# GpSimd's gathers of five passes wait for the sum three turns back in place of four

## The reference

```
agg = segment_sum(edge_attr, dst);  x = LN(x + x + W2 softplus'(W1 agg))          # layer 0
neigh = segment_sum(x[src]*ew, dst) / max(ws, 1)
x = LN(x + (x Wself + neigh Wneigh + b)/2)                                       # layer 1
x = LN(x + relu(x w_s + segment_sum((x w_n)[src], dst)))                         # layer 2
h = relu(cheb(x; T0, T1 = lap(x), T2 = 2 lap(lap(x)) - x))                       # layer 3
x = LN(x + cheb(h))
lap(h) = segment_sum(w * h[src], dst)
```

## Time and profile before

| what | us |
|---|---|
| median of 3 runs (4736.85 to 4740.95) | 4739.85 |
| the profiled execution, its own time | 4710.22 |
| its span, first to last instruction | 4708.4 |
| L1, from its first gather to that of L2 | 327.0 |
| L2 | 313.5 |
| T1 | 315.6 |
| T2 | 319.8 |
| LH | 325.4 |
| LU, to the end | 567.2 |

### The profile page before, as it was taken

One profiled execution on the slowest core, in us unless ns is written; L12 is line 12 of the kernel. 1 busy time (PEld: TensorE's weight loads), 2 busy tenths in 40 slices (PEclk: granted clock), 3 DMA queues, 4 the chain that ended last, 5 costly groups with the idle time before them and its releaser, 6 DMA issues. The chain is left out here.

```text
span 4708.4 us, 74947 instructions
## 1 busy us (share of the span) xinstructions
PE 3333.1 (71%) x20670; PEld 2616.6 (56%) x20670; DVE 3087.9 (66%) x12832; ACT 2498.5 (53%) x7359; POOL 3171.7 (67%) x3630
## 2 busy tenths in 40 slices
PE   2266986777999999999995664666868878831111
PEld 0023655665888888888884564653436667721111
DVE  2277996997888888888885775771213434545544
ACT  0002776997888888888884552114545643311111
POOL 6402767885888888888885664656656646566776
PEclk6598998998999999999997777888999988955555
DMA  0003663664222222222222443435657766632332
GB/s 21 4 1 92 185 178 123 214 215 149 78 76 75 77 78 78 76 75 78 78 78 67 127 134 100 134 123 176 227 176 255 268 205 209 215 111 91 90 88 70
DMA packets 311878, 575.84 MB, mean 122 GB/s; under 512 B 69502, under 2 KB 97975, under 8 KB 311466
## 3 DMA queue, kind: packets, MB, share of 16 engines
q1 hardware_dynamic: 235178, 443.56, 28.0%
q0 software_dynamic: 76288, 127.51, 10.1%
HBM read 301.23 MB, written 271.14 MB: 122 GB/s over the span
## 5 line engine op out<-in xcount | busy, mean ns | idle before, releaser
L561 POOL DMA_INDIRECT rows<-state,rows_of_src x588 | 555.8, 945 | 390.5 <-issue 155.0
L844 DVE TENSOR_TENSOR_SCAN x<-same,x,ps 128x512 f32<-128x512 uint8 x336 | 429.0, 1277 | 319.2 <-PE ps L1360 205.2
L1360 PE MATMUL ps<-ident,rows 128*128 128x128 f32 x1372 | 287.2, 316 | 460.9 <-ACT rows L1130 250.0
L1113 ACT ACTIVATE yTa<-ps 128x512 f32<-128x512 f32 x392 | 232.8, 594 | 602.8 <-PE ps L1342 338.7
L561 POOL DMA_INDIRECT rows<-lap,rows_of_lap x392 | 383.4, 978 | 218.2 <-issue 109.9
L1360 PEld LDWEIGHTS ps<-ident,rows 128*128 128x128 f32 x1372 | 202.2, 165 | 510.7 <-issue 304.6
L645 POOL DMA_INDIRECT lk<-node_table,look_idx x392 | 388.9, 992 | 92.2 <-issue 84.1
L1130 ACT ACTIVATE rows<-rows,lap_w 128x128 f32<-128x128 f32 (+1 forms) x784 | 269.6, 418 | 278.0 <-DMA rows<-lap,rows_of_lap 211.1
L1118 ACT ACTIVATE sd<-mv,consts 128x4 f32<-128x4 f32 x588 | 174.6, 297 | 438.0 <-DVE mv L856 172.9
L1498 PE MATMUL ps<-V,hT 128*128 128x128 f32 x3136 | 403.2, 282 | 5.0 <-ACT hT L1249 5.0
L960 DVE BATCH_NORM_STATS2 bn<-y 128x6 f32<-128x128 f32 x1764 | 379.6, 278 | 23.3 <-POOL y L597 23.2
(11 more groups left out here) (259 smaller groups left out, 9473.4 us busy)
## 6 DMA issues: line engine op xcount, KB each, us to landing
state_h<-hb SPq DMA_DIRECT2D x98, 512.0 KB
xin<-in_x_dram SPq DMA_DIRECT2D x196, 256.0 KB
out_dram<-outb SPq DMA_DIRECT2D x196, 256.0 KB
xe<-state SPq DMA_DIRECT2D x147, 256.0 KB
state<-outb SPq DMA_DIRECT2D x98, 256.0 KB
state<-oe SPq DMA_DIRECT2D x98, 256.0 KB
h_pre<-hb SPq DMA_DIRECT2D x49, 512.0 KB
rows<-in_edge_attr_10x_dram SPq DMA_DIRECT2D x48, 320.0 KB
```

What stands on the lines that cost most here:

```text
L561: gp.indirect_dma_start(out=dest[:, at, k, 0:width], out_offset=None, in_=table_, in_offset=bass.IndirectOffsetOnAxis(ap=index[:, c:c + 1] ...
L844: v.tensor_tensor_scan(t[0:np_, g.b].rearrange("p k d -> p (k d)"), same[0:np_, 512 * g.c:512 * g.c + 512], ps[0:np_, bk + g.b, :], t[0:np ...
L1360: i = t.transpose(bank(g.b)[:, k, :], rows[:, g.r, k, 0:P], ident[:, :])
```

## The change

One number: in the passes L1, L2, T1, T2 and LH turn g's gathers wait for `summed` of turn g - 3, not g - 4. The four buffers stay. Turn g writes buffer g modulo 4 as before, so the new wait is stricter than what the buffer needs. LU, tgt0 and src0 are as they were.

```diff
             def edge_pass(p, table_, index, width=P):
                 enter(pool, p)
-                run_turns(QUADS, 0, lambda g: gather(p, g, table_, index, rows, g.r, width, rows_in, [(summed, RING)]))
+                run_turns(QUADS, 0, lambda g: gather(p, g, table_, index, rows, g.r, width, rows_in, [(summed, 3)]))
                 leave(pool)
```

## The result

| | us |
|---|---|
| before, median of 7 runs | 4738.60 |
| after, median of 7 runs (4706.15 to 4724.60) | 4720.86 |
| after / before | 0.9960, 95% interval 0.9944 to 0.9975 |
| predicted | 4718.5 |

What follows compares the result with a forecast made beforehand. POOL's gathers, with stops for PE's late-seen sums, were taken as the bound. Start -27.0, middle +29.9, end -24.3 sum to -21.4 us, taking 4739.85 to 4718.5; by itself 4708 to 4730, overall range 4708 to 4747.

Steps and rivals of the forecast that it cites:

- The cause of the stall: At pass starts, POOL's unbroken gathers hold PE's signals; four passes stop after 24 gathers and restart at about 34 us.
- the first rival: At pass starts, the stall has a cause other than POOL's gathers, so the restart stays put: 4740 us, chance 0.19.
- the backlog: In POOL's unbroken gathers, a queue said to hold PE's signals until drained; each further gather costs 1.35 us.
- The start: First stall of each pass: POOL stops four gathers earlier, release comes 5.4 us sooner; five passes save 27.0 us.
- the middle: From restart to last turn: one more turn of each pass runs at the coupled pace, +29.9 us in all.
- the end: After each pass's last gather: one turn fewer remains at PE's own pace, -24.3 us in all.
- POOL and PE keep their rhythm: In the middle of each pass: same rhythm, only with gathers one turn less ahead; the added coupled turns cost +29.9 us.
- the second rival: In L2, T1 and T2, two turns and a stop become one turn and a stop: 12 us cost, 4730.5, chance 0.07.
- Rows in time: At LH's weighing, rows need 7.55 us and have 8.5 us of cover; that leaves 1 us, cost taken 0.
- The third rival: At ACT's weighing in LH and L1, rows come late: 4750 to 4790 us, chance 0.11.

Runs made afterwards that it cites:

- e1: The change as it is (three turns back in the five passes) against the kernel before, on another chip: 1.0006 (0.9997 to 1.0016).
- e7: Kernel before (four turns back), with PE's four products of each sum in the five passes done three times over: 1.0189 of the kernel before.
- e8: Three turns back, with PE's four products of each sum in the five passes done three times over: 1.0185 of the kernel before.
- e10: Only the sixth turn of each pass waits three back, all others four, against the kernel before (4699.0 us): 0.9991 (0.9981 to 1.0001).
- e12: First twelve turns of each pass wait four back, from the thirteenth three back, against the kernel before (4746.2 us): 0.9983 (0.9971 to 0.9995).
- e9: Kernel before (four turns back) plus two small POOL settings behind each gather of the five passes, against the kernel before (4699.0 us): 1.0039.
- e11: Kernel before (four turns back) plus four small POOL settings behind each gather of the five passes, against the kernel before (4746.2 us): 1.0057.
- e6: All five passes wait two turns back, against the kernel before, on a prompt chip: 1.0312 (1.0294 to 1.0331).

## Why the prediction came out, point by point

**The cause of the stall** held on the chip where it was made. Signals of PE are late because POOL issues DMAs without a break: this was argued from four times of 34 us. The change itself bears it out, since the restart moved with the count in all five passes, 27.1 us in sum for 27.0 (in T2 to 33.6 us, after 24 gathers), and with that the first rival fell there. The loop beside the puts shows the lateness where nothing joins the two engines. That the signals come through once POOL is silent and the backlog drained is one step too much: beside the puts they come through every 28 us or oftener with POOL going on, and what holds them stays open. And the rival holds on the other chips (e1, e7, e8), and that a chip might be of another kind was in none of my cases.

**The start, the middle and the end belong together**: e10 has the early restart without the rest, and gives at most 9 us; the whole change gives 0.4%. But e12, which should have cost 0 to 12 us, gained 2 to 14. On its chip about 8 us are there without the start, where the whole change gave 18 on the first, by a gain in LH that my sum doesn't have.

**"POOL and PE keep their rhythm"** is the step that was off, in both directions, and hence the middle's +29.9 us, which measured +42.5. A turn more is 5.0 us of gathers and whatever the stops change. POOL's waits from the restart to the last turn, before and then after, in L1:

```profile
POOL rows L561 <- PE ps L1360: 43.4, 17, 4.4
POOL rows L561 <- remote: 13.0, 6, 4.3
```

```profile
POOL rows L561 <- PE ps L1360: 52.0, 17, 4.0
...
POOL rows L561 <- remote: 15.4, 9, 3.8
```

and in LH:

```profile
POOL rows L561 <- remote: 41.1, 28, 4.4
...
POOL rows L561 <- PE ps L1364: 25.9, 12, 3.5
```

```profile
POOL rows L561 <- remote: 51.1, 38, 2.1
...
POOL rows L561 <- PE ps L1364: 11.8, 5, 4.1
```

L1 has 56.4 us of stops before and 67.4 after: 11.0 + 5.0 = 16.0 us, where I had 6.1. LH has 67.0 and 62.9: -4.1 + 5.0 = 0.9, where I had 6.2. In LH before, each of the five stretches of two turns ends in a stop of 1.7 to 1.9 us and the turn behind it in one of 2.2 to 3.2, among single turns with 1.0; after, 42 of 44 stretches of gathers are single turns. That is the second rival's mechanism, and I had priced it as a loss, from the earlier trace rows and for other passes (12 us; with the 4.69 + 1.28 = 5.97 us that stand there it would be 14 to 15). In LH, where most turns were single already, it was a gain of 5.3 us. e12 shows it again, and e9 with four turns back, so that it goes with the rhythm rather than with the distance. What makes a pass settle in single turns is not shown. L1's loss of 9.9 us is not settled: its turn took 6.10 and 6.03 us with four back (before, e10) and 6.33 and 6.60 with three (after, e12). But these are single executions of several chips, and with four back and the settings it took 6.31 in e11 and 6.5 in e9. So L1 differs by as much from trace to trace without the change, and its +9.9 can't be put down to it.

**The end** was sized within a tenth in sum, -26.7 for -24.3, by errors that cancel: L1 had 0.9 us less than its term, T1 and T2 1.3 and 2.0 more.

**Rows in time**: nearly right for three back. The 1 us of slack in LH was read well, and it was used up: from the restart on ACT has 12 waits ahead of its weighing in after, 10.5 us in sum and none above 1.3, where before it had none. The pass became shorter all the same. The third rival's place was thus right. With two turns back (e6, on a prompt chip) late rows cost 138 us in the passes; that L1 would fall deepest was not seen.

The errors of the middle (+12.6) and the end (-2.4) leave the trace at -11.3 us for -21.4. The medians say -17.7, with an interval of -12 to -27; -21.4 lies in it, and the sum of this one pair of traces, which may be of two chips, just outside. The profiled execution did not go from 4710.2 to 4688.8 us but to 4724.6, with 24.3 us of the difference ahead of L1. And no pass did what was forecast for it: each should have been 4 to 5 us shorter. LH gained 9.0 by something that the sum has not, L1 lost 6.8, the other three gained about 3 each. That 4720.9 stands so close to 4718.5 is luck; the mechanism of the start and of the end is not.

## What to carry to other kernels

When a consumer resumes long after its producer's record has ended, and a third engine that issues indirect DMAs falls silent just before, look for a loop elsewhere in the trace that shares no data with that engine: if it slows as well, the signal is held and the work is not late. A shorter wait at one place alone gains nothing, since it is eaten at the next turn. Look at the rhythm too: what a pass gains can come from pairs of turns that break up into single ones, and a sum of mean turns doesn't see that. Don't read a pass's gain of some us off one pair of traces: L1, four turns back (with POOL's settings and without), took from 325 to 348 us. And time such a change on several chips, since what it acts on may exist on some of them only.

## What was not expected of the hardware

- The same program takes 4265 to 4267 us on two chips and 4699 to 4746 on the others, at the same pace in the dense stage (1492.1 and 1493.1 us). 391 of the 457 us between two traces lie in the puts and the five passes, where POOL's indirect DMAs follow one another closely. What makes a chip late, these runs don't say.
- Beside the puts of a late chip the held signals came through in a beat of 28 us, with POOL issuing all the while.
- On a late chip PE and DVE, in a loop of their own, did a tenth of their work beside POOL's puts (12 products in 40 us against 121), and the granted clock there was 0.50, that is 1.2 GHz, against 1.00 on the prompt chip: on top of its waits PE ran at the lower level.
- A setting of one column takes POOL 0.05 to 0.12 us and costs nothing behind a gather, up to two of them: pitch 1.25 us with none, one and two, 1.30 with four.
- On a late chip POOL was held without a wait of its own after 14 to 16 gathers with four settings each, and after 21 or 22 with two.
